# A slot of a software-pipelined attention kernel: scores and the transposition of probabilities ahead of all three projections

## What is computed

```python
def attn_layer(x, Wqkv, qs, ksc, Wo):          # HEADS = 16, DIM_HEAD = 64
    q, k, v = jnp.split(x @ Wqkv, 3, -1)       # then cut into heads
    q = l2norm(q) * qs
    k = l2norm(k) * ksc
    q = q * cos * scale + rotate_half(q) * sin * scale
    k = k * cos * inv + rotate_half(k) * sin * inv
    # local_attention: windows of 32 queries see their own 32 keys and the 32 before
    sim = jnp.einsum('bhwie,bhwje->bhwij', bq, bk2) * QK_SCALE
    sim = jnp.where(mask, -jnp.finfo(sim.dtype).max, sim)
    attn = jax.nn.softmax(sim, -1)
    out = jnp.einsum('bhwij,bhwje->bhwie', attn, bv2)
    return out @ Wo                            # heads merged again
def ffn_layer(x, g, bln, W1, b1, W2, b2):
    hg = xn @ W1 + b1                          # xn: layer norm of x
    a, gate = jnp.split(hg, 2, -1)
    return a * jax.nn.gelu(gate, approximate=False) @ W2 + b2
for i in range(DEPTH):                         # DEPTH = 6
    x = attn_layer(shift_tokens(x), ...) + x
    x = ffn_layer(shift_tokens(x), ...) + x
```

## Time and profile before

| | |
|---|---|
| median of 3 runs | 1763.3 us (1762.95 to 1766.94) |
| the profiled execution's own time | 1763.62 us |
| its span | 1761.8 us |
| mean granted TensorE clock | 0.988 |
| PE busy | 1647.7 us, 94% |
| PE weight loads busy | 1294.0 us, 73% |
| DVE busy | 1434.6 us, 81% |
| ACT busy | 1338.1 us, 76% |
| POOL busy | 1310.0 us, 74% |
| DMA | 66.40 MB, mean 38 GB/s |

### The profile page before, as it was taken

How to read it: one execution, slowest core, us unless ns; L and a number is a source line. 1 busy time by engine, 2 the same in 40 slices (tenths; PEclk the granted TensorE clock), 3 DMA queues, 4 the chain that set the end, 5 groups by cost and what they waited for, 6 DMA issues and landing times.

```text
span 1761.8 us, 68566 instructions
## 1 busy us (share of the span) xinstructions
PE 1647.7 (94%) x25968; PEld 1294.0 (73%) x26160; DVE 1434.6 (81%) x3011; ACT 1338.1 (76%) x2661; POOL 1310.0 (74%) x1305
## 2 busy tenths in 40 slices
PE   6789999999999999999999999999999999999995
PEld 5667777777777777777777777777777777777773
DVE  4499888888888888888888888888888888888875
ACT  4267878787877878787787778778777877777785
POOL 6187877777777777777777777777777777777765
PEclk9799999999999999999999999999999999999998
DMA  5011111111111111111111111111111101111000
GB/s 155 30 31 43 34 33 40 31 42 44 34 31 30 37 37 39 48 30 31 30 36 42 48 36 30 31 30 48 38 40 36 30 27 37 35 30 31 28 23 25
DMA packets 41425, 66.40 MB, mean 38 GB/s; under 512 B 7072, under 2 KB 16032, under 8 KB 41376
## 3 DMA queue, kind: packets, MB, share of 16 engines
q1 hardware_dynamic: 40224, 65.38, 12.4%
q10 hardware_dynamic: 1152, 0.34, 0.1%
HBM read 20.61 MB, written 1.05 MB: 12 GB/s over the span
## 4 chain that ended last, share of the span: by engine, by line
PE 86%; ACT 5%; issue 4%; DVE 4%; DMA 0%; ACTq 0%; POOL 0%; DVEq 0%; POOLq 0%
PE ps_qs L529 12%; PE ps_a L529 12%; PE ps_po L529 11%; PE ps_q L529 10%; PE ps_v L529 7%; PE ps_k L529 7%; PE ps_f L529 7%; PE ps_po L648 6%; PE ps_tk L639 5%; PE ps_qs L639 5%; PE ps_tk L529 4%; ACT q_t L937 1%; ACT k_t L937 1%; ACT squares L943 1%; DVE qk_rot L1246 1%
## 5 line engine op out<-in xcount | busy, mean ns | idle before, releaser
L426 POOL TENSOR_TENSOR qk<-qk,rnorm 128x512 f32<-128x512 f32 x384 | 393.0, 1044 | 200.9 <-DVE rnorm L1272 200.3
L418 POOL TENSOR_TENSOR qk<-qk,qk_rot 128x512 f32<-128x512 f32 x384 | 483.2, 1280 | 0.0
L1277 DVE TENSOR_REDUCE row_max<-ps_qs 128x8 f32<-128x512 f32 x191 | 131.9, 691 | 209.6 <-PE ps_qs L529 209.4
L937 ACT COPY p_bd<-ps_po 64x512 f32<-64x512 f32 x378 | 218.9, 579 | 91.1 <-PE ps_po L648 88.7
L937 ACT COPY attn_t<-ps_po 128x512 f32<-128x512 f32 x191 | 113.0, 592 | 207.9 <-PE ps_po L529 207.9
L433 POOL TENSOR_TENSOR prob<-prob,row_inv 128x512 f32<-128x512 f32 x192 | 200.4, 1044 | 93.9 <-DVE row_inv L1289 93.9
L1252 DVE TENSOR_REDUCE ssq<-squares 128x8 f32<-128x512 f32 x384 | 261.1, 680 | 3.4 <-ACT squares L943 3.4
L529 PE MATMUL ps_qs<-k_t,q_t 64*32 64x64 f32 x12224 | 210.3, 218 | 31.1 <-issue 30.9
L529 PEld LDWEIGHTS ps_qs<-k_t,q_t 64*32 64x32 f32 x12224 | 179.5, 107 | 43.5 <-issue 43.5
L529 PE MATMUL ps_po<-p_bd,v_back 128*64 128x64 f32 x3056 | 193.2, 225 | 0.0
L529 PEld LDWEIGHTS ps_po<-p_bd,v_back 128*64 128x64 f32 x3056 | 162.9, 137 | 35.9 <-issue 17.0
(11 more groups left out here) (234 smaller groups left out, 3966.2 us busy)
## 6 DMA issues: line engine op xcount, KB each, us to landing
v_back<-v_own SPq DMA_DIRECT2D x192, 192.0 KB, 2.4
w_raw<-in_wqkv SPq DMA_DIRECT2D x48, 192.0 KB, 2.4
v_back<-v_own SPq DMA_DIRECT2D x96, 64.0 KB, 2.1
wo_sb<-in_wo SPq DMA_DIRECT2D x12, 256.0 KB, 3.0
w_sb<-in_w SPq DMA_DIRECT2D x6, 341.0 KB, 3.2
w_sb<-in_w SPq DMA_DIRECT2D x6, 192.0 KB, 2.6
x_in<-in_x SPq DMA_DIRECT2D x4, 256.0 KB, 4.4
out<-s_out SPq DMA_DIRECT2D x8, 128.0 KB, 1.9
```

Source lines behind the costliest of these rows:

```text
L418: nc.gpsimd.tensor_tensor(qk[:, s, i, :], qk[:, s, i, :], qk_rot[:, s, i, :], ALU.add).then_inc(added, 1)
L426: nc.gpsimd.tensor_tensor(heads(qk[:, s, i, :]), heads(qk[:, s, i, :]), rnorm[:, s, 8 * i:8 * i + 8].unsqueeze(2).to_broadcast([P, 8, HEAD ...
L937: return nc.scalar.copy(o, i)
L1277: V.tensor_reduce(row_max[:, s, :], heads(ps[:]), AX, ALU.max).then_inc(max_done, 1)
```

## The change

Inside PE's body the projection of q moves from the head of the slot behind scores and turn_p, directly ahead of the projections of k and v. Each of the four slots and all 48 batches have this order. The other engines' queues, the drain, all semaphores and what each operation waits for stay as they are.

```diff
             def body(n):
                 for j in range(UNITS):
                     u = UNITS * n + j
-                    project(n, j, 0, ps_q, q_scaled, q_done)
                     if live(u - 3):
                         scores(u - 3, (j - 3) % UNITS, (j - 3) % 2)
                     if live(u - 4):
                         turn_p(u - 4, j % 2)
+                    project(n, j, 0, ps_q, q_scaled, q_done)
                     project(n, j, 1, ps_k, k_scaled, k_done)
```

## The result

| | before | changed |
|---|---|---|
| median | 1764.98 us (4 runs) | 1872.55 us (4 runs, 1867.79 to 1878.95) |
| profiled execution, own time | 1763.62 us | 1873.76 us |
| span | 1761.8 us | 1872.0 us |
| mean granted TensorE clock | 0.988 | 0.954 |
| one steady batch | 34.35 us | 35.55 us at full clock, 37.04 to 37.26 us with a fall of the clock |

The changed kernel is slower: ratio 1.061, 95% interval 1.058 to 1.065.

What follows compares the result with a forecast made beforehand. PE, holding 86% of the chain that ended last, was taken as the bound. The profiled 1763.6 us plus 72 for the schedule and 60 for clock falls gave 1895.6, stated as 1895 us; range 1824 to 1915.

Steps and rivals of the forecast that it cites:

- its likeliest case: Stall in slot 1 plus clock falls nearly everywhere: 1895 us, own range 1875 to 1912, chance 0.58.
- both large terms: Schedule of the steady batches, +72 us, and clock falls after slot 1's idle stretch, +60 us.
- part 1: PE, every slot: one bare projection entry fewer, saving 0.11 us a slot, bounds 0 and 0.22.
- part 2: ACT, every slot: squares of q wait for the later q, starting 2.80 us into the slot, with ACT's queue behind.
- part 3: Slot 1: ACT's gapless queue moves ff_down to 8.69 us; +1.66 us a slot, idle stretch 2.4 us.
- part 4: Slot 2 into slot 3: scores wait 0.3 us for slot 2's k_t, +0.2 us against before.
- part 5: PE's clock falls after slot 1's idle stretch in 40 of 44 batches, 1.5 us each: +60 us.
- Rival A: PE's clock holds and only the stall is paid: 1835 us (1820 to 1848), chance 0.24.
- Rival B: Faster: PE's entry saved, ACT's delay never shows at ff_down (k_t shift under 0.33 us): 1743 us, chance 0.04.
- Rival C: k_t 0.5 us late in slots 0 and 3 too: 44 us more at worst, about 1915 with falls, chance 0.06.

Runs made afterwards that it cites:

- the run with slots 0, 2 and 3: New PE order (q's projection behind scores and turn_p) in slots 0, 2 and 3 only, slot 1 old, against the kernel before: 1767.2 us, ratio 1.0015.

## Why the prediction was right, point by point

The forecast was 1895 us and the range held the time; its likeliest case is the one that came, and both large terms were a little too big: +72 and +60 us, against 53 and 53. What is left of the 110 us, some 4, lies in the start-up and the end: the first ff_down comes 211.83 - 209.18 = 2.65 us later, about 1 us more than its own slot's stall explains.

**The entry (part 1)** held: k's first piece is followed after 0.24 us, the mask keeps 0.32, slot 0 is 8.51 instead of 8.61 us. The row was the right guide. What the sum missed is the loop's edge, some 0.2 us in slot 3, on top of the 0.11. The Trainium skill's rule of weight loads pulled ahead ("TensorE: Matmul & The Clock Gate", "Part 2: What happens when you issue a matmul") would have left both entries free; the trace of the changed kernel disagrees at q's first piece again, 0.32 us against 0.23 to the next, and its load starts at 1087.69, beside the matmul at 1087.72.

**ACT behind q (part 2)** held: squares start at 2.74 us of the slot (2.80 forecast). DVE's newton was priced at nothing. It does wait, 190.2 us in all, and POOL behind it waits longer too; that reaches nobody on PE, whose waits in the steady batches name k_t alone. I had seen that gelu ends late in slot 0 only as a matter of turn_p; the carry-over to slot 1 was not in the working. In the full change it is hidden, since ACT waits there for q anyway, and so the forecast didn't suffer; my next expectation, for slots 0, 2 and 3, did.

**Slot 1 (part 3)** held to 0.1 us: ff_down at 8.61 us (8.69), the slot 11.00 (11.08), the idle stretch 2.33 (2.4). The table load is followed by Ln 1090.61 - 1089.32 = 1.29 us after its start, so the drain of 1.38 us that the Trainium skill adds ("ScalarE: Activation LUTs", "What ACT_TABLE_LOAD costs") is not seen here either.

**Slot 2 into 3 (part 4)** is a term that was mis-sized. Slot 2 takes 7.45 us, 0.05 above before and not 0.2. The steps on ACT held (Ln follows squares by 0.49 us, keep_p follows lnt by 0.31), but squares start 0.06 us earlier than forecast, the sum had been rounded up by some 0.04 on its way, and PE starts 0.15 us after k_t's end and not 0.2. Together, per batch: slot 1 -0.08 against the forecast, slot 2 -0.15, slot 3 -0.22, slot 0 +0.01, which makes 0.44 us or 19 of the 72 us.

**The clock (part 5)** held in kind: both longer idle stretches of the earlier trace rows were followed by the low level and so are most of the new ones. The share was 34 of 44 batches, not 40 (33 of the 43 distances and the last batch, whose ff_down lasts 1.95 us), and the price 1.5 to 1.7 us, not 1.5. The share had been taken from two early stretches alone; that it came so near is partly luck, for no part of the working gives the ten batches that hold. Rival A (the clock holds) is what the kernels with added matmuls give: 1818 to 1820 us, at the lower end of A's own range or just below it. Rival B's point, a shift of k_t under 0.33 us, was right in kind: the run with slots 0, 2 and 3 has a shift of 0.4 us and ends level. Rival C didn't come: slots 0 and 3 have no wait.

## What to carry to other kernels

Before an operation is moved back on the busiest engine, look at who waits for its result and what stands behind that waiter in its queue: here 1.6 us of delay for one small read went through the rest of ACT's queue for that slot and came back to TensorE. The same move is a gain of 1.5% once the waiter's queue is put in the order in which its inputs now arrive. When a stall grows, read from the trace after which idle lengths the clock has fallen before, and price both together; a few dummy matmuls in the stretch tell the two costs apart.

## What the runs showed of the hardware that was not expected

The clock's reaction to the length of the stretch has an edge: 0 of 43 batches at 1.77 us of idle and 33 of 43 at 1.99 us. The length isn't all, since 10 of 43 batches hold with 2.33 us. They don't come at random: every fourth or fifth batch holds. These are ff_down of four batches of the changed kernel in a row, and one of the kernel with slot 1 alone changed:

```profile
1130.13 2.46 PE L529 MATMUL ps_tk<-ff_m,w_sb 128*64 128x257 f32 x12 [2.34 <-ACT k_t L937]
1167.29 2.09 PE L529 MATMUL ps_tk<-ff_m,w_sb 128*64 128x257 f32 x12 [2.34 <-ACT k_t L937]
1204.41 1.68 PE L529 MATMUL ps_tk<-ff_m,w_sb 128*64 128x257 f32 x12 [2.34 <-ACT k_t L937]
1241.45 1.52 PE L529 MATMUL ps_tk<-ff_m,w_sb 128*64 128x257 f32 x12 [2.33 <-ACT k_t L937]
```

```profile
1074.91 2.84 PE L529 MATMUL ps_tk<-ff_m,w_sb 128*64 128x257 f32 x12 [2.33 <-ACT k_t L940]
```

The idle stretch is the same, but the low clock catches less of ff_down each time, about 0.4 us less of stretching per batch, and the fourth of these holds (1241.45 to the next ff_down are 35.54 us). With slot 1 alone changed the batches come 37.5 us apart instead of 37.1, ff_down lasts 2.82 to 2.84 us in 42 of 44 batches, and all 43 fall. So which batch falls goes with where in time its stretch lies, besides how long it is; why the distance of 37.5 us never misses the runs don't show.

At the hardware loop's edge TensorE lost some 0.2 us when a projection of q with its wait for the new batch came first behind the branch, and not when the mask did. The kernel before shows it by itself. In the 41 batches at whose end the loop goes round, slot 3 lasts 8.86 to 8.95 us; in batch 4, which is unrolled, and in the loop's last pass it lasts 8.69:

```profile
218.98 0.50 PE L529 MATMUL ps_q<-w_hi,xs_hi 128*128 128x512 f32 x1
227.67 0.50 PE L529 MATMUL ps_q<-w_hi,xs_hi 128*128 x1
```

Which instruction of the edge costs it was not tried.
